# Experts' token rows gathered straight into SBUF, and the overflow rows loaded in batches

## What is computed

```
ys = y / sqrt(512);  d = rsqrt((ys*ys) @ (weight*weight) + 1e-8)
xf = (x * ys) @ weight * d
top1 = argmax(softmax(xf @ gate_w.T))            # one expert of 2 for each token
masked_e = xf where top1 == e, else 0            # zero rows still pass through the expert's biases
routing = sum_e( relu(masked_e @ w1[e] + b1[e]) @ w2[e] + b2[e] )
shared = relu(xf @ sw1 + sb1) @ sw2 + sb2
out = x + routing + shared
```

## Time and profile before

| | |
|---|---|
| median of 3 runs | 1418.56 us (1415.41 to 1419.16) |
| the profiled execution | 1417.61 us |
| its span, first to last instruction | 1415.8 us |
| PE busy | 1384.6 us, 98% |
| DVE, ACT, POOL busy | 64%, 45%, 20% |
| DMA, mean | 224 GB/s |
| mean granted clock of TensorE | 0.991 of full |

### The profile page before, as it was taken

How to read it: one execution, slowest core, us unless ns; L and a number is a source line. 1 busy time by engine, 2 the same in 40 slices (tenths; PEclk the granted TensorE clock), 3 DMA queues, 4 the chain that set the end, 5 groups by cost and what they waited for, 6 DMA issues and landing times.

```text
span 1415.8 us, 17098 instructions
## 1 busy us (share of the span) xinstructions
PE 1384.6 (98%) x6086; PEld 1142.5 (81%) x6086; DVE 904.4 (64%) x1313; ACT 643.6 (45%) x929; POOL 282.3 (20%) x260
## 2 busy tenths in 40 slices
PE   9999999999799999999899999999999999999995
PEld 8888888888677888888788888888888888888884
DVE  7979967667497746675468868786866334333330
ACT  4456644445256556765566444544643221222220
POOL 0000005435343300000000000010011133166665
PEclk9999999999899999999999999999999999999998
DMA  6967485889999765633557888889897655366653
GB/s 203 300 227 230 172 258 192 254 276 312 343 351 349 268 173 193 194 134 119 184 192 276 273 270 255 289 270 301 272 276 260 195 154 164 116 160 171 159 132 59
DMA packets 223925, 317.65 MB, mean 224 GB/s; under 512 B 51440, under 2 KB 98544, under 8 KB 223824
## 3 DMA queue, kind: packets, MB, share of 16 engines
q1 hardware_dynamic: 200528, 267.06, 58.0%
q0 software_dynamic: 22016, 47.00, 12.3%
q10 hardware_dynamic: 1296, 2.49, 0.5%
HBM read 184.47 MB, written 140.90 MB: 230 GB/s over the span
## 4 chain that ended last, share of the span: by engine, by line
PE 54%; DMA 6%; POOL 4%; issue 3%; DVE 1%; ACT 0%; ACTq 0%; POOLq 0%; DVEq 0%
PE bank L1935 22%; PE bank L1859 19%; PE bank L1964 12%; DMA loose_rows<-x_rows,tab_in 6%; POOL loose_rows L846 2%; POOL out L832 2%; POOL xr L826 1%; PE bank L1878 1%; DMA hidden_scratch<-vb 0%; DMA loose_hidden<-hu 0%; PE bank L1981 0%; PE bank L1977 0%; DVE rows L1338 0%; DVE vb L1407 0%; ACTq L1055 0%
## 5 line engine op out<-in xcount | busy, mean ns | idle before, releaser
L1859 PE MATMUL bank<-xw,w_hi 128*128 128x512 f32 x1792 | 557.1, 392 | 13.6 <-issue 6.4
L1859 PEld LDWEIGHTS bank<-xw,w_hi 128*128 128x128 f32 x1792 | 338.1, 189 | 87.2 <-issue 8.4
L1374 DVE TENSOR_TENSOR hl<-hin,hl 128x512 fp32r<-128x512 f32 x352 | 236.9, 690 | 262.6 <-ACT hl L965 258.5
L965 ACT CAST hl<-hin 128x512 fp32r<-128x512 f32 x352 | 217.6, 624 | 385.8 <-PE bank L1964 214.2
L1859 PE MATMUL bank<-xw,w_lo 128*128 128x512 f32 x896 | 350.7, 391 | 0.0
L1964 PE MATMUL bank<-w_hi,hl 128*128 128x512 f32 x1024 | 315.5, 389 | 0.0
L1935 PE MATMUL bank<-hl,w_hi 128*128 128x512 f32 x896 | 275.9, 389 | 0.0
L1964 PEld LDWEIGHTS bank<-w_hi,hl 128*128 128x128 f32 x1024 | 192.2, 188 | 39.9
L1964 PE MATMUL bank<-w_lo,hl 128*128 128x512 f32 x512 | 199.2, 389 | 0.0
L1859 PEld LDWEIGHTS bank<-xw,w_lo 128*128 128x128 f32 x896 | 169.4, 189 | 35.8
L1935 PEld LDWEIGHTS bank<-hl,w_hi 128*128 128x128 f32 x896 | 168.2, 188 | 34.9
(11 more groups left out here) (184 smaller groups left out, 1200.1 us busy)
## 6 DMA issues: line engine op xcount, KB each, us to landing
hin<-hidden_scratch SPq DMA_DIRECT2D x112, 512.0 KB
hidden_scratch<-vb SPq DMA_DIRECT2D x80, 512.0 KB
hin<-expert_hidden SPq DMA_DIRECT2D x64, 512.0 KB
expert_hidden<-vb SPq DMA_DIRECT2D x48, 512.0 KB
hidden_scratch<-vt SPq DMA_DIRECT2D x32, 512.0 KB
w_new<-w_shared SPq DMA_DIRECT2D x52, 256.0 KB, 5.3
sorted_scratch<-sorted_rows POOLq DMA_DIRECT2D x48, 256.0 KB
ring<-x_cols SPq DMA_DIRECT2D x32, 256.0 KB, 5.4
```

The lines of the kernel that those rows point to most:

```text
L965: nc.scalar.copy(hl[:, n % HL, 0, :], hin[:, n // 2 % LOADS, n % 2, :]).then_inc(hu_hi, 1)
L1374: nc.vector.tensor_tensor(hl[:, n % HL, 1, :], hin[:, n // 2 % LOADS, n % 2, :], hl[:, n % HL, 0, :].bitcast(F32), ALU.subtract).then_inc( ...
L1859: last = nc.tensor.matmul(up_bank(u, UP_BANK[c])[p][:], w[:, DOWN_W[c], pair, part], xw[:, c, x, k, :], start=(c in FRESH and n == 1), sto ...
```

## The change

1. The 32 tiles of the expert blocks are no longer copied. A table `quad_tab` holds, for each partition (quarter q, lane b), the row 4t + q of `xf_scratch` for each token; it is made once by 16 small copies and three additions on POOL. For each of blocks 4 to 7 POOL then issues 32 gathers (`gather_rows`), one for each piece j: 128 rows of 512 bytes straight into `rows`. SP's `next_rows` serves only the shared blocks.
2. A flip of an expert block waits only for its eight gathers. Flips 0 and 1 stay at the start of group 2, flip 2 goes before the last adds of the group, flip 3 behind them.
3. Only the 16 overflow tiles go through `sorted_rows`, now two buffers, and their gathers leave out padding rows. They stand in front of the gathers of blocks 4, 5 and 6 (6, 5 and 5 tiles). ACT still waits for them at group 20.
4. In a loose unit ACT issues the next unit's row loads first, and no longer waits at the end for its own store. The signal `loose_up_done` comes from ACT one group later, behind the take of that group's first bank.
5. At the end SP loads four overflow tiles at a time (`loose_load`), before units 4 to 7, and POOL gathers x onto them with an add, then scatters them. `loose_in_rows` and `loose_at` are gone.

```diff
-SORT = (*range(KD * W), *range(NT, COLS), *range(KD * W, NT))
+SPILL_TILES = CAP // P
+SORT_WAITS = (*(10 * PER_GROUP + 5 * k for k in range(6)), *(14 * PER_GROUP + 8 + 4 * k for k in range(5)),
+              *(18 * PER_GROUP + 8 + 3 * k for k in range(5)))
+SORT_BEFORE = {BLOCKS - 1: (0, 6), BLOCKS: (6, 11), BLOCKS + 1: (11, 16), BLOCKS + 2: (16, 16)}
...
             def sort_in(k):
 
-                i, u = k % RING, SORT[k]
-                pool.wait_ge(up_mm, PER_GROUP * SORT_GROUP + 2 * k)
-                wait(pool, sorted_out[i], DMA * (k // RING))
-                pool.indirect_dma_start(sorted_rows[i][:], None, xf_rows,
-                                        bass.IndirectOffsetOnAxis(tab_in[:, u:u + 1], 0)).then_inc(sorted_in[i], DMA)
+                i, u = k % 2, NT + k
+                pool.wait_ge(up_mm, SORT_WAITS[k])
+                wait(pool, sorted_out[i], DMA * (k // 2))
+                pool.indirect_dma_start(sorted_rows[i][:], None, xf_rows, bass.IndirectOffsetOnAxis(tab[:, u:u + 1], 0),
+                                        bounds_check=N - 1, oob_is_err=False).then_inc(sorted_in[i], DMA)
...
+            def gather_rows(s):
+
+                pool.wait_ge(xw_lo, STEPS * s)
+                for j in range(JW):
+                    if (s - 1) * GROUPS == LOOSE_UP[0] and j == JW // 2:
+                        pool.wait_ge(loose_up_done, 2)
+                    u, a = (s - BLOCKS) * JW // W + j // W, j % W
+                    pool.indirect_dma_start(rows[:, j, :], None, xf_dram,
+                                            bass.IndirectOffsetOnAxis(quad_tab[:, a, u:u + 1], 0)).then_inc(rows_sorted[j // (JW // FLIPS)], DMA)
+
+            for s in range(BLOCKS - 1, UPS - 1):
+                for k in range(*SORT_BEFORE[s]):
+                    sort_in(k)
+                    if k > 0:
+                        sort_out(k - 1)
+                    if k == SPILL_TILES - 1:
+                        sort_out(k)
+                gather_rows(s + 1)
...
@@ SP @@
+            def loose_load(batch):
+
+                if batch == 0:
+                    sp.wait_ge(loose_down_done, 2)
+                    sp.wait_ge(loose_filled, DMA * (2 + SPILL_TILES))
+                for i in range(RING):
+                    k = RING * batch + i
+                    sp.wait_ge(sorted_out[i], DMA * (sorts_of[i] + batch))
+                    sp.dma_start(loose_rows[i][:], loose_out[k * P:(k + 1) * P, :]).then_inc(ring_in[i], DMA)
...
+                batch, at = divmod(n - PAIRS * (LOOSE_DOWN[0] + 1) - LOADS + 1, PAIRS)
+                if at == 0 and 0 <= batch < SPILL_TILES // RING:
+                    loose_load(batch)
...
@@ POOL, the last loop @@
-                if k == 0:
-                    pool.wait_ge(loose_down_done, 2)
-                if 0 <= k - 2 < CAP // P:
+                beside = 0 <= k < SPILL_TILES
+                if beside and k % RING > 1:
                     loose_out_rows(k - 2)
-                if 0 <= k - 1 < CAP // P:
-                    loose_add_rows(k - 1)
+                if beside:
+                    loose_add_rows(k)
                 scatter(u)
                 if u + XR < NT:
                     gather_xr(u + XR)
-                if 0 <= k < CAP // P:
-                    loose_in_rows(k)
+                if beside and k % RING == RING - 1:
+                    loose_out_rows(k - 1)
+                    loose_out_rows(k)
...
@@ ACT @@
+                if u - 1 in LOOSE_UP:
+                    e = LOOSE_UP.index(u - 1)
+                    units = spilled[0] if e == 0 else spilled[0] + spilled[1]
+                    act.wait_ge(loose_kept, units * (2 * DMA) + 1)
+                    nc.scalar.copy(primed[:], ones[:, 0:1]).then_inc(loose_up_done, 1)
...
+                act.wait_ge(loose_lo, 2 * x + 2)
+                loose_rows_load(x + 1)
+                act.wait_ge(loose_kept, 2 * DMA * x + 1)
                 for q in range(QUADS - 1):
                     flat(q)
...
                 loose_rows_hi(x + 1)
-                act.wait_ge(loose_kept, 2 * DMA * (x + 1))
...
@@ DVE @@
-                dve.wait_ge(rows_in, QD * DMA * (s + 1))
+                if s < BLOCKS:
+                    dve.wait_ge(rows_in, QD * DMA * (s + 1))
+                else:
+                    dve.wait_ge(rows_sorted[i], DMA * JW // FLIPS * (s - BLOCKS + 1))
```

More of the change, by code:

```diff
@@ L63 @@
 SCATTER_GROUP = 6
-SORT_GROUP = 10
 KB = 256
@@ L542, in raw_load @@
                 if n == RAW_LAST:
-                    for i in range(RING):
-                        sp.wait_ge(sorted_out[i], DMA * COLS // RING)
+                    for i in range(FLIPS):
+                        sp.wait_ge(rows_sorted[i], DMA * JW // FLIPS * BLOCKS)
                 if n == RAW_LAST + 1:
@@ L573, in next_rows @@
                 sp.wait_ge(xw_lo, STEPS * (s + 1))
-                if s + 1 >= BLOCKS and q == 0:
-                    tiles_done = SORT.index(W * 2 * (s + 2 - BLOCKS) - 1) + 1
-                    for i in range(RING):
-                        sp.wait_ge(sorted_out[i], DMA * (tiles_done // RING))
-                if s * GROUPS == LOOSE_UP[0] and q == 0:
-                    sp.wait_ge(loose_up_done, 2)
                 sp.dma_start(rows[q * B32:(q + 1) * B32, :, :], quad_rows(q, s + 1)).then_inc(rows_in, DMA)
@@ new lines, in _ @@
+            pool.wait_ge(tab_ready, 2)
+            for q in range(QD):
+                for a in range(W):
+                    pool.dma_start(quad_tab[q * B32:(q + 1) * B32, a, :], tab_quads[a * B32:(a + 1) * B32, :]).then_inc(tab_dma, DMA)
+            pool.wait_ge(tab_dma, DMA * (2 + QD * W))
+            for q in range(1, QD):
+                part = quad_tab[q * B32:(q + 1) * B32, :, :]
+                pool.tensor_scalar(part, part, q, None, ALU.add).then_inc(tab_ready, 1)
+                pool.wait_ge(tab_ready, 2 + q)
@@ L811, in sort_out @@
-            def sort_out(k):
-                i = k % RING
-                pool.wait_ge(sorted_in[i], DMA * (k // RING + 1))
-                pool.dma_start(sorted_tile(SORT[k]), sorted_rows[i][:]).then_inc(sorted_out[i], DMA)
-            for k in range(COLS + 2):
-                if k < COLS:
-                    sort_in(k)
-                if k >= 2:
-                    sort_out(k - 2)
+                i, u = k % 2, NT + k
+                pool.wait_ge(up_mm, SORT_WAITS[k])
+                wait(pool, sorted_out[i], DMA * (k // 2))
@@ L1097, in _ @@
                     if u == LOOSE_UP[0] and not spilled:
-                        for i in range(RING):
-                            act.wait_ge(sorted_out[i], DMA * COLS // RING)
+                        for i in range(2):
+                            act.wait_ge(sorted_out[i], DMA * SPILL_TILES // 2)
                         act.wait_ge(pick_ready, 1)
@@ L1108, in _ @@
                             loose_rows_hi(0)
+                            nc.scalar.copy(primed[:], ones[:, 0:1]).then_inc(loose_kept, 1)
                         with act.If(spilled[e] > 0):
@@ L1420, in up_group @@
                 if g == 2 and s < UPS - 1:
-                    for i in range(FLIPS):
+                    for i in range(FLIPS if s < BLOCKS - 1 else 2):
                         flip(s + 1, i)
@@ L1451, in up_group @@
                     x_sum_of(s + 1, 3)
+                if g == 2 and BLOCKS - 1 <= s < UPS - 1:
+                    flip(s + 1, 2)
                 add(u, vt1, 5, 4, 0)
@@ L1467, in up_group @@
                     make_t3(u)
+                if g == 2 and BLOCKS - 1 <= s < UPS - 1:
+                    flip(s + 1, 3)
                 if u == RANK_GROUP:
```

67 lines of the change are left out of this document (30 added, 37 removed).

## The result

| | before | after |
|---|---|---|
| median | 1418.86 us (1415.41 to 1423.42, 4 runs) | 1396.66 us (1395.97 to 1400.46, 4 runs) |
| ratio | | 0.985, 95% interval 0.9827 to 0.9874 |

The change makes the kernel 22.2 us faster. The forecast was 1395 us, with a range of 1388 to 1406, so time and range held. The sum behind it did not hold in every term: one loss that I had left to a rival came true, and the gain in the stretch 300 to 500 us is larger than I had it. Of the kernel before, one of the executions timed beside experiments 1 to 4 took 4986 us and enters no comparison.

The account below looks back on a forecast made before the run. PE's matmuls were taken as the bound, busy 98% of the span. From 1417.6 us, tail -8.1, loose unit -5.0, copy traffic -13.0 and gathers +3.0 gave 1394.5, with the offset to the median 1395 us; range 1388 to 1406.

Parts of the forecast that it names:

- What bounds the kernel: Whole kernel: PE's matmuls bound it, busy 98%; only 31.2 us of standstill and half-clock stretches can be gained.
- Tail: End of the program: with rows loaded by SP in batches, POOL's last scatter follows DVE's last add closely, -8.1 us.
- Loose unit: 666 to 692 us: moving ACT's wait for hu removes 3.3 us of PE gap and 1.7 of half clock, -5.0 us.
- Copy traffic: 300 to 500 us: 32 tiles no longer copied, less traffic, 13.0 of the 16.0 us PE loses come back.
- Gathers in rows: Boundaries of the four expert blocks: 32 gathers per block at 1.36 to 1.46 us nearly fit, +3.0 us for all.
- Flips: Expert blocks: splitting the flips moves two of them in DVE's row but adds none; no time given.
- Rival 1: Group 20: ACT newly waits for all 16 overflow tiles, PE loses 0 to 11 us plus 1.7; 1402 us, chance 0.20.
- Rival 2: 300 to 500 us: store waits stay because SP's own stores fill the DMA engines; 13 us don't come, 1408, chance 0.10.
- Rival 3: Block boundaries: POOL becomes the bound with gathers over 1.46 us; at 1.7 us 38 us more, 1433, chance 0.04.
- Rival 4: End of the program: the tail doesn't shorten, POOL still ends late because of the batches' waits; 1403 us, chance 0.06.
- The rule against it: POOL's gathers: VectorE holding the shared port makes transfers some 3100 ns, 32 gathers about 100 us, sum over 1500 us.

Follow-up runs that it names:

- late wait: Changed kernel with ACT's wait for the 16 overflow tiles moved from the head of group 20 to behind its third bank's take and last split: 1389.14 us, as control 1388.71.
- experiment 4: Kernel before with only ACT's part of the loose unit changed (row loads first, no wait for its own store, signal one group later): 1415.05 us, ratio 0.997.
- experiment 1: The changed kernel run again as it is, nothing edited: 1396.09 us, ratio 0.9849 to the kernel before.
- experiment 5: late wait with 27 memory-to-memory copies of 512 KB (14.2 MB) added on ACT's queue in groups 11 to 19: 1392.3 us in the second run.
- experiments 1 and 2: The changed kernel run again unedited, 1396.09 us, and the late wait, 1389.14 us.
- point 8: First runs on one chip of late wait with copies, flips together, or one memset per gather: 1490.1, 1484.3, 1416.7 us; kernel before there 1416.1.
- experiment 3: Kernel before with only the end changed (SP loads overflow tiles in batches, POOL's new last loop): 1409.93 us, ratio 0.9948.

## Why the prediction was right, and where it was not

Against the profile of before, the control of the late wait has a span 27.9 us shorter, and three places make it: (878 - 812) x 0.2266 = 15.0 us between 300 and 500 us, 5.2 at the loose unit (between the two matmuls of experiment 4) and 8.0 in the tail. They add up to 28.2. The changed kernel gives 7.0 of it back at group 20, and its profiled execution another 3.7 at block 4.

- **What bounds the kernel**: right. PE's busy time fell by 4 us, in which it had run at half clock; the rest was time in which it stood still.
- **Tail, -8.1 us**: -8.0. Before, a tile took POOL 9.3 to 9.7 us, not the 10 to 11 of my working, so it did gain on PE's 10.9, but from too late a start. In the profile after, POOL finishes the overflow at 1370.36 + 1.82 and issues its last scatter at 1392.66, 0.9 us behind the end of DVE's last add (1391.10 + 0.69), not the 0.3 to 0.5 I had named. SP's wait in front of the batches came out at the 5 us forecast, and no gap of PE follows:

```profile
SPq L701 <- DMA out<-loose_rows,tab: 14.7, 4, 4.9
```

- **Loose unit, -5.0 us**: 5.2 in the trace of the changed kernel, 4.8 alone; by the medians 2.9, since the old tail took back 1.9 (experiment 4). The step is right. ACT still waits 1.24 us for hu, now behind the take:

```profile
678.45 0.19 ACT L1026 COPY primed<-ones 128x1 f32<-128x1 f32 x1 [1.24 <-DMA loose_hidden<-hu]
```

- **Copy traffic, -13.0 us**: the direction is right, the size came from the right rows, and two things in it were off. The part of 3.0 us that I left for DVE's own load went too (1.0 us is left of the 16.0), so the term was 15.0. And the bytes were wrong: I forecast 8.8 MB and 220 GB/s for 345 to 385 us, and it is 11.9 MB and 298 GB/s, since PE no longer stands still there and the stores that were held up are issued as well. A DMA rate beside a stall is not the load that the kernel wants; it is what got through. That the *volume* was the cause is not borne out: experiment 5 put 14.2 of the 16.8 MB back and cost 3.4 us. What it was beside the volume is not shown.
- **Gathers in rows, +3.0 us**: mis-sized; near nothing in the profiles of experiments 1 and 2 (PE loses under 1 us at each boundary), 3.7 in the profile after (experiment 1). The pace was inside or below the bracket of 1.36 to 1.46 us (1.25 to 1.46 by block), and the limit was right, about 4 us into the fourth group. The start was not. I wrote that the table copies and the first overflow tiles delay something "for which nobody waits yet"; but the gathers of block 4 stand behind those tiles in POOL's queue. They begin 16.5 us into block 3 in the slow execution and 12.4 in the next, not 11.1. For block 5 they begin 12.8 to 13.5 us in. DVE takes up nearly all of a wait of flip 3 of 4.3 us at block 5, but the 3.49 us at block 4 PE paid one for one. In the late wait flip 3 starts at the limit for block 4 and 0.9 us behind it for block 5, so this is a narrow pass.

```profile
L844 POOL DMA_INDIRECT rows<-xf_scratch,quad_tab x128 | 135.2, 1056 | 94.2 <-DVE xw L1376 56.1 <-issue 37.8 <-PE bank L1896 0.3
```

- **Flips, "adds none"**: true of the work, but I took it for granted and named no price for leaving it out. It is what makes the gathers affordable: without it 46.5 us are lost.
- **Rival 1, chance 0.20**: this is the step that failed, and in its chance, not its price. The text had 0 to 11 us and 1.7 of half clock; measured are 5.1 and 3.1, 7.0 by the medians. A store let its gather go after 3.2 to 4.0 us, inside my bracket of 2.5 to 5.1. But the bracket itself said more than I took from it: 56 + 4 x 1.8 + 4 + 5 x 2.9 is 81.7, so PE waits from 2.9 us on, and only the lowest sixth of the bracket is free of a gap. Two sizes in the sum were off in opposite directions. Block 5's gathers ended 59.8 us into block 4 and not at 56, and from there to the last landing it took 26.0 us, near the low end of 24 to 37, because only four of the five tiles wait for a store. Together 85.7 us, 4 behind the 81.6 from which PE waits; the issue of the four loads, 1.85 us, which stands between that landing and the take, I had left out. The rival was the likelier case and belonged in the sum. That the total still fits is luck: 7.0 us lost here stand against 5.0 that the two terms above had too little.
- **Rival 2** (store waits stay, 1408): no. DVE has one of 4.2 us left between 340 and 400 us. **Rival 3** (gathers over 1.46 us): not by the pace, but the place where it bites is real; a late start cost 3.7 us once, and at 1.45 to 1.65 us a gather the boundaries cost 12.2. **Rival 4**: no.
- **The rule against it** (the Trainium skill, SBUF — State Buffer, "SBUF: two separate sides", with its 3100 ns for a transfer beside VectorE's copies): the trace does not show it here. 128 gathers beside a DVE that is busy 65% of the span have a mean of 1056 ns; a median of 947 and a longest of 2913 ns. Single ones come near the figure, the mean does not. DVE's work beside them was additions and transposes, and no copy of the kind of which that section speaks, so the rule itself is not tested. On the one chip of point 8 it was not the gathers that were slow either, but everything else.

## What to carry to other kernels

When rows arrive by many small gathers, take the time of the *last* landing and put each consumer behind work that does not need it: the order of four transposes decided between 1389 and 1435 us. Count also what stands ahead of the first gather in its queue. An in-order engine that waits for a far-off transfer should do so behind the take that releases the bound engine's buffers; the same five lines moved within one group were worth 7 us. And where a bracket crosses the point from which a wait decides, the chance is the share of the bracket beyond that point, not a feeling about traffic.

## What the runs showed of the hardware

- An indirect transfer of 128 rows costs POOL about the same for rows of 512 B (1056 ns in the mean) as before for 2 KB (1106, a gather) and 64 B (1159, a scatter), with 0.3 us between. Small rows are paid for in number, not in bytes.
- 14.2 MB of large copies beside the stores (DMA share 1.02, 374 GB/s) lengthened landings (weights 10.6 us against 6.1) but cost PE only 2.3 us by the trace, 3.4 by the medians.
- A gap of PE of about 3.3 us has a half clock of 3.4 us behind it in the profile before and none in that of experiment 3, at the same place; a gap of 5.1 us had one of 6.8 us in both profiles.
- One chip, at one time, differed from the others by far more than 0.3% on some kernels and not on another: 49 us for the kernel with flips together, 98 us for the one with copies, 0 to 2 us for the kernel before.
